# First layer of a two-layer decoder on one core: taps in one bank, skip row on TensorE, first pair first, diagonals on GpSimd

## The reference

```
scores = (x Wq)(ctx Wk)' / sqrt(32)          # 4 heads, 154 keys
top    = the 32 largest scores of each row; softmax over them, 0 elsewhere
c      = mean over heads (probs) @ (ctx Wv) * text_mask
u      = layernorm(x) * (1 + gate * scale_in(c)) + gate * shift_in(c)
K[d,l] = 2 Re sum_n dC[d,n] exp(dt[d] A[d,n] l),  l = 0..511      # the taps
y      = causal convolution of u with K (by FFT) + D_skip * u
out    = layernorm(x + film_out(y) + FFN(...))
```

## Time and profile before

| | us |
|---|---|
| median of 3 runs | 796.4 (796.21 to 798.48) |
| profiled execution, time | 798.87 |
| profiled execution, span on the core | 797.0 |
| TensorE matmuls busy in the span | 715.0 (90%) |
| VectorE busy | 456.8 (57%) |
| ScalarE busy | 279.4 (35%) |
| GpSimd busy | 225.4 (28%) |

### The profile page before, as it was taken

The page is one execution under the profiler, slowest core; times in us unless marked ns, Lnnn a source line. Parts: engine busy times, 40 slices in busy tenths (PEclk is TensorE's granted clock), DMA queues, the critical chain, the costliest instruction groups (busy, mean ns, idle before and its releaser), DMA issues.

```text
span 797.0 us, 8521 instructions
## 1 busy us (share of the span) xinstructions
PE 715.0 (90%) x3088; PEld 355.8 (45%) x3088; DVE 456.8 (57%) x1192; ACT 279.4 (35%) x527; POOL 225.4 (28%) x134
## 2 busy tenths in 40 slices
PE   8756869798989999999999999989968999999996
PEld 4223456774845443222222222228433354656555
DVE  7698973422635785576766767734664635333333
ACT  7799754003021003544444444430214103121220
POOL 4726910000200020445354545550725010000001
PEclk9757989999998999999999999999988969999999
DMA  8100050020000000000000000000500000000000
GB/s 313 32 0 0 1 211 2 1 81 27 1 0 1 0 1 0 0 1 1 0 1 1 1 0 1 0 1 1 225 0 1 1 0 0 2 1 1 0 1 27
DMA packets 3491, 18.64 MB, mean 23 GB/s; under 512 B 887, under 2 KB 2040, under 8 KB 2938
## 3 DMA queue, kind: packets, MB, share of 16 engines
q1 hardware_dynamic: 3450, 18.11, 5.9%
HBM read 17.58 MB, written 0.52 MB: 23 GB/s over the span
## 4 chain that ended last, share of the span: by engine, by line
PE 68%; DVE 14%; ACT 9%; issue 3%; POOL 3%; DMA 1%; POOLq 0%; DVEq 0%; SPq 0%; ACTq 0%
PE PS L1847 10%; PE PS L1330 7%; PE PS L1861 5%; DVE SB L1484 5%; PE PS L1314 4%; PE PS L1285 4%; PE PS L1298 3%; PE PS L217 3%; DVE SB L1233 2%; PE PS L1346 2%; PE PS L704 2%; PE PS L1368 2%; PE PS L1413 2%; PE PS L1645 2%; PE PS L1656 1%
## 5 line engine op out<-in xcount | busy, mean ns | idle before, releaser
L197 POOL TENSOR_TENSOR SB<-SB 128x4 f32<-128x4 f32 (+1 forms) x24 | 23.9, 996 | 374.4 <-DVE SB L181 374.3
L1467 POOL TENSOR_TENSOR SB<-SB 128x1024 f32<-128x1024 f32 x32 | 75.2, 2349 | 127.8 <-ACT SB L1437 127.7
L1484 DVE TENSOR_REDUCE SB<-PS 128x2 f32<-128x1024 f32 x64 | 78.5, 1226 | 52.7 <-PE PS L1298 52.7
L1437 ACT ACTIVATE SB<-PS 128x1024 f32<-128x1024 f32 x64 | 65.5, 1023 | 105.3 <-PE PS L1317 105.2
L217 PE MATMUL PS<-SB 128*128 128x512 f32 (+1 forms) x190 | 89.7, 618 | 8.3 <-ACT SB L536 6.7
L1847 PE MATMUL PS<-SB 128*128 128x512 f32 x176 | 83.9, 618 | 0.0
L1314 PE MATMUL PS<-SB 64*128 64x512 f32 x256 | 68.9, 616 | 0.0
L1330 PE MATMUL PS<-SB 128*64 128x512 f32 x256 | 67.8, 610 | 1.2 <-DVE SB L1521 1.2
L1927 DVE TENSOR_TENSOR SB<-SB,PS 128x512 f32<-128x512 f32 (+1 forms) x48 | 33.0, 688 | 53.9 <-PE PS L1847 50.0
L1517 DVE RECIPROCAL SB<-PS 128x512 f32<-128x512 f32 x16 | 53.7, 3358 | 17.6 <-PE PS L1346 17.6
L1885 ACT ACTIVATE SB<-PS 128x512 f32<-128x512 f32 (+1 forms) x48 | 28.6, 596 | 88.6 <-PE PS L1847 88.6
(11 more groups left out here) (355 smaller groups left out, 1145.7 us busy)
## 6 DMA issues: line engine op xcount, KB each, us to landing
SB<-exp SPq DMA_DIRECT2D x1, 4352.0 KB, 14.0
SB<-moe SPq DMA_DIRECT2D x1, 4096.0 KB, 12.1
SB<-dft SPq DMA_DIRECT2D x1, 2304.0 KB, 11.8
SB<-att SPq DMA_DIRECT2D x1, 2048.0 KB, 7.9
SB<-mix SPq DMA_DIRECT2D x1, 768.5 KB, 4.8
SB<-mix SPq DMA_DIRECT2D x1, 640.0 KB, 6.0
SB<-ssm SPq DMA_DIRECT2D x1, 602.0 KB, 7.0
SB<-lat SPq DMA_DIRECT2D x1, 585.0 KB
```

What stands on the lines that cost most here:

```text
L1437: act.activation(expd[i % 2][:, 1024 * u:1024 * u + 1024], bank(2 * (u % 2), 2), ACT.Exp).then_inc(sem("d_exp"), 1)
L1467: pool.tensor_tensor(half_sums[half], e[:, 0:1024], e[:, 1024:], ALU.add).then_inc(sem("d_half_sum"), 1)
L1484: dve.tensor_reduce(shift[i % 2][:, qt:qt + DK + 1:DK], two_heads(bank(4, 2)), AX_X, ALU.max, negate=True)\
```

## The change

- Taps: one matmul for each of the 128 channels, 32 stationary columns (low lags) by 16 moving ones (high lags), placed at column group 32 j of the array (j = d mod 4), all written to bank 3. Their waits for ScalarE's copies of gathers and films and the wait of `gather(5)` for the copies of the taps go. ScalarE's 16 copies read bank 3.
- Skip: GpSimd halves D early (`b_pool_pre`), and TensorE adds the row to tap 0 by one matmul of one partition in each of the 8 groups of the taps' spectrum, which moves from behind `gather(5)` to behind `gather(6)`.
- Selection: VectorE selects pair 0 before it finds the peaks of pair 2; ScalarE copies the second scores after the exponentials of pair 1. The last round writes to bank 2 only.
- Diagonals: GpSimd forms the four diagonals of a tile by one product, placed among its products of the taps. ScalarE's `b_act_spectrum` moves behind the loop.

```diff
@@ -352,7 +352,8 @@
     minus_max, total, share = Sel(NT * H_X), Sel(NT * H_X), Sel(NT * H_X)
     exp_ring, left_ring, prob_ring = Sel(8 * S2), Sel(4 * S2), Sel(8 * S2)
     all_exp, left, probs = ([a[:, S2 * i:S2 * i + S2] for i in range(n)] for a, n in ((exp_ring, 8), (left_ring, 4), (prob_ring, 8)))
-    diag = [Sel(128) for _ in range(4)]
+    diagonal = Sel(H_X * 128)
+    diag = [diagonal[:, 128 * h:128 * h + 128] for h in range(H_X)]
 
     scored = [d_tab[:, 0:H_X * S2], d_tab[:, H_X * S2:2 * H_X * S2]]
     attn0 = Sel(T)
@@ -466,13 +467,6 @@
         pool.wait_ge(sem("s_low_waves"), h + 1)
         pool.tensor_tensor(low_k[:, c], low_k[:, c], low_e[:, c], ALU.mult).then_inc(sem("s_low_products"), 1)
 
-    def b_dve_skip(dve, follow):
-
-        dve.wait_ge(sem("s_taps_copied"), 16)
-        dve.wait_ge(sem("small_in"), SMALL)
-        follow(dve.tensor_scalar(skip_line, skip_line, 0.5, None, ALU.mult))
-        dve.tensor_tensor(taps[0:1, 0:128], taps[0:1, 0:128], skip_line, ALU.add).then_inc(sem("s_taps_in"), 1)
-
     def b_act_spectrum(act):
 
         act.wait_ge(sem("s_taps_dft"), 1)
@@ -529,11 +523,11 @@
     def b_act_taps(act):
 
         act.wait_ge(sem("s_taps"), 1)
-        tp = PS[:, 2048:4096].rearrange("p (g j c q) -> p c g j q", j=4, c=4, q=4)
+        tp = bank(3).rearrange("p (g c q) -> p c g q", c=4, q=4)
         to = taps.rearrange("p (c g j) -> p c g j", c=4, j=4)
         for q in range(4):
             for j in range(4):
-                act.activation(to[32 * q:32 * q + 32, :, :, j], tp[32 * j:32 * j + 32, :, :, j, q], ACT.Copy)\
+                act.activation(to[32 * q:32 * q + 32, :, :, j], tp[32 * j:32 * j + 32, :, :, q], ACT.Copy)\
                    .then_inc(sem("s_taps_copied"), 1)
 
     def b_pe_values(pe):
@@ -620,6 +614,7 @@
         for h in range(2):
             pool.tensor_copy(m2[:, :, h, :], by_batch)
         follow(pool.tensor_copy(ones_low, ones[0:1, :]))
+        follow(pool.tensor_scalar(skip_line, skip_line, 0.5, None, ALU.mult))
         follow(pool.tensor_copy(text_mask, text_bytes))
         pool.tensor_scalar(text_mask, text_mask, 1.0 / H_X, None, ALU.mult).then_inc(sem("masks_in"), 1)
         pool.wait_ge(sem("masks_in"), 1)
@@ -668,24 +663,21 @@
 
         def taps_of_lags():
 
-            pe.wait_ge(sem("x_attn_in"), 2 * TAPS_AT)
-            pe.wait_ge(sem("x_film_in"), TAPS_AT - 1)
             pe.wait_ge(sem("s_low_products"), 5)
             pe.wait_ge(sem("s_factors"), 4)
-            for g in range(D // 4):
-                ins = pe.matmul(PS[:, 2048 + 4 * HIGH * g:2048 + 4 * HIGH * (g + 1)], low_k[:, 4 * LOW * g:4 * LOW * (g + 1)],
-                                high_r[:, 4 * HIGH * g:4 * HIGH * (g + 1)], start=True, stop=True)
+            for d in range(D):
+                j, g = d % 4, d // 4
+                ins = pe.matmul(bank(3)[32 * j:32 * j + 32, HIGH * g:HIGH * g + HIGH], low_k[:, LOW * d:LOW * d + LOW],
+                                high_r[:, HIGH * d:HIGH * d + HIGH], start=True, stop=True, tile_position=(0, 32 * j))
             ins.then_inc(sem("s_taps"), 1)
 
         def gather(t):
 
             if t >= 2:
                 pe.wait_ge(sem("x_attn_in"), 2 * (t - 1))
-            if t == TAPS_AT:
-                pe.wait_ge(sem("s_taps_copied"), 16)
             stay_warm(pe, 1, 4 + t % 2)
             pe.wait_ge(sem("x_probs"), 2 * t + 2)
-            pe.wait_ge(sem("x_diag"), H_X * t + H_X)
+            pe.wait_ge(sem("x_diag"), t + 1)
             o = bank(4 + t % 2)
             for h in range(H_X):
                 i = H_X * t + h
@@ -721,14 +713,15 @@
         def taps_spectrum():
 
             pe.wait_ge(sem("x_scores_in"), NT)
-            pe.wait_ge(sem("s_taps_in"), 1)
+            pe.wait_ge(sem("s_taps_copied"), 16)
             pe.wait_ge(sem("dft_in"), 16)
             for part, mat in ((0, dft["dft_cos"]), (1, dft["dft_sin"])):
                 for j in range(4):
+                    o = bank(part)[:, 128 * j:128 * j + 128]
                     for c in range(4):
-                        ins = pe.matmul(bank(part)[:, 128 * j:128 * j + 128],
-                                        mat[:, 512 * c + 128 * j:512 * c + 128 * j + 128],
-                                        taps[:, 128 * c:128 * c + 128], start=(c == 0), stop=(c == 3))
+                        ins = pe.matmul(o, mat[:, 512 * c + 128 * j:512 * c + 128 * j + 128],
+                                        taps[:, 128 * c:128 * c + 128], start=(c == 0), stop=False)
+                    ins = pe.matmul(o, mat[0:1, 128 * j:128 * j + 128], skip_line, start=False, stop=True)
             ins.then_inc(sem("s_taps_dft"), 1)
 
         score(0)
@@ -749,7 +742,7 @@
                     for j in range(4):
                         spectrum(0, j, 0)
                 film_tile(k)
-            if t == TAPS_AT:
+            if t == TAPS_AT + 1:
                 taps_spectrum()
         pe.wait_ge(sem("s_u_late"), 1)
         pe.wait_ge(sem("x_film_in"), NT)
@@ -776,7 +769,7 @@
             two = (2 * j, 2 * j + 1)
             m8 = [best[:, TOP * i:TOP * i + TOP] for i in two]
             base = 12 * j
-            rest = bank(2 + j % 2)[:, 0:2 * S2]
+            rest = bank(2)[:, 0:2 * S2]
             if j >= 2:
                 dve.wait_ge(sem("x_probs"), j - 1)
             for k, i in enumerate(two):
@@ -790,6 +783,8 @@
                     dve.wait_ge(sem("x_best"), base + 4 * r + k - 1)
                     if r == 3 and i == 0:
                         dve.wait_ge(sem("x_small_in"), 6)
+                    if r == 3 and j >= 1:
+                        dve.wait_ge(sem("x_probs"), j)
                     to = rest[:, S2 * k:S2 * k + S2] if r == 3 else left[i % 4]
                     ins = dve.match_replace(to, m8[k][:, 8 * r:8 * r + 8], left[i % 4], 0.0)
                     ins.then_inc(sem("x_selected" if r == 3 else "x_best"), 1)
@@ -801,7 +796,7 @@
             if i >= 8:
                 dve.wait_ge(sem("x_gathered"), i // 4 - 1)
             dve.tensor_tensor(prob_ring[:, S2 * (i % 8):S2 * (i % 8) + 2 * S2], exp_ring[:, S2 * (i % 8):S2 * (i % 8) + 2 * S2],
-                              bank(2 + j % 2)[:, 0:2 * S2], ALU.subtract).then_inc(sem("x_probs"), 1)
+                              bank(2)[:, 0:2 * S2], ALU.subtract).then_inc(sem("x_probs"), 1)
 
         def shares(t):
 
@@ -818,15 +813,15 @@
         peak(0)
         peak(1)
         for j in range(PAIRS_X):
-            if j + 2 < PAIRS_X:
+            if 0 < j < PAIRS_X - 2:
                 peak(j + 2)
             select(j)
+            if j == 0:
+                peak(2)
             if j % 2 == 0:
                 selected(j)
             else:
                 shares(j // 2)
-            if j == 14:
-                b_dve_skip(dve, follow)
 
     def b_act_attention(act):
         def scores_in(t):
@@ -847,17 +842,6 @@
                 act.activation(all_exp[i % 8], scores(i), ACT.Exp, bias=bias).then_inc(sem("x_exp"), 1)
                 act.activation(best[:, TOP * i:TOP * i + 8], peaks[:, 8 * i:8 * i + 8], ACT.Exp, bias=bias).then_inc(sem("x_exp"), 1)
 
-        def diagonals(t):
-            act.wait_ge(sem("x_sums"), 2 * t + 2)
-            act.activation(share[:, H_X * t:H_X * t + H_X], total[:, H_X * t:H_X * t + H_X], ACT.Copy, scale=text_mask[:, t:t + 1])\
-               .then_inc(sem("x_share"), 1)
-            act.wait_ge(sem("x_share"), t + 1)
-            if t >= 1:
-                act.wait_ge(sem("x_gathered"), t)
-            for h in range(H_X):
-                i = H_X * t + h
-                act.activation(diag[h], ident, ACT.Copy, scale=share[:, i:i + 1]).then_inc(sem("x_diag"), 1)
-
         def film_in(t):
             act.wait_ge(sem("x_film"), t + 1)
             if t == 0:
@@ -865,16 +849,12 @@
             act.activation(film[:, 512 * t:512 * t + 512], bank(6 + t % 2), ACT.Copy).then_inc(sem("x_film_in"), 1)
 
         scores_in(0)
-        scores_in(1)
         exponentials(0)
         b_act_film_inputs(act)
         exponentials(1)
+        scores_in(1)
         b_act_film_rows(act)
         for t in range(NT):
-            if t >= 1:
-                diagonals(t - 1)
-            if t == NT - 1:
-                b_act_spectrum(act)
             if t + 1 < NT:
                 exponentials(2 * t + 2)
             if t + 2 < NT:
@@ -896,7 +876,7 @@
                 b_act_low_rates(act, 16, LOW)
             if t == 3:
                 b_act_high_rates(act)
-        diagonals(NT - 1)
+        b_act_spectrum(act)
         film_in(NT - 2)
         attn_in(act, NT - 1)
         for k in FILMS[NT - 1]:
@@ -911,6 +891,18 @@
 
     def b_pool_attention(pool, follow):
         every_row = lambda a: a[:, None, :].to_broadcast([P, NT, 128])
+
+        def diagonals(t):
+            h = slice(H_X * t, H_X * t + H_X)
+            pool.wait_ge(sem("x_sums"), 2 * t + 2)
```

(27 more changed lines are left out.)

## The result

The changed kernel takes 805.3 us in the median, beside 800.1 us of the kernel before on the same chip: a ratio of 1.0061, with a 95% interval of 1.0040 to 1.0083, so 4.9 us slower (3.2 to 6.6). Six of its 20 executions (811.4 to 814.4 us) ran over 1.5% longer than its fastest and are left out of the ratio; without them the median is 804.8. The profiled execution took 805.25 us with a span of 803.5; the one of before 798.87 and 797.0.

What follows compares the result with a forecast made beforehand. VectorE's selection was taken to bound the stage's first half, TensorE's order its end from the taps on. +7.5 + 8.7 - 6.75 - 1.8 + 4.7 = +12.4 us gave 808.8 us, range 798 to 822.

Steps and rivals of the forecast that it cites:

- GpSimd's diagonals: First layer's cross-attention and filter: diagonals queue behind GpSimd's products, gathers wait, and the taps start 7.5 us later, at 108.3.
- Rival C: GpSimd is not in the way: gathers 1 to 3 not delayed, taps start at 100.8; 801.3 us, chance 0.10.
- The taps: TensorE: 256 loads and 256 small matmuls take 16.0 us (0.0625 each) against 7.33 now, +8.7, all on the path.
- Rival B: TensorE's column groups overlap: 7.2 us for the taps, +3.6 in all, 800.0 us; chance 0.13.
- Rival D: Small matmuls cost next to nothing (taps 3.5 us) and one-row matmuls hide (1.8): -3.0 us, 793.4 us; chance 0.10.
- The wait that goes: TensorE before the warming matmul at 114.68: ScalarE's copies no longer hold `gather(5)`, -6.75 us.
- The half clock behind the hole: Warming matmul and gather behind TensorE's removed wait no longer run at granted clock 0.50: -1.8 us.
- First pair first: VectorE's pair 0 starts 3.3 us earlier; some 2 us stay, eaten by the wait for `gather(1)`.
- Skip row: Taps' spectrum on TensorE: one-row matmuls add 0.59 us per group, 8 groups, +4.7 us on the path.
- The sum in the stage: First layer's cross-attention and filter: all terms together +12.4 us, L704's last piece starting at 159.3 against 146.9.
- The path from the stage to the end: What comes after L704's closing 96 instructions hangs on them and moves with them.
- rival A: Small matmuls go no faster than L1079's: 28.7 us for the taps, +25.1 in all, 821.5 us; chance 0.17.

Runs made afterwards that it cites:

- taps_twice: The changed kernel with the 128 matmuls of the taps done twice over, to the same places; 807.0 us in one execution.

## Why the prediction was right or wrong

The direction held, and the time (805.3) lies in the range. Two things make that look better than it is. I had forecast +12.4 us and it is +4.9; the 808.8 is near only because it starts from 796.4, while the kernel before took 800.1 beside the changed one. And 805.3 falls into the part of the range, 804 to 815, that I had tied to taps of 12 to 22 us. The taps took 4.7, under the 8 us below which I had called the prediction wrong. By its own test the mechanism of the largest term failed, and the nearness of the time is luck. By the steps:

- **GpSimd's diagonals: right.** Taps predicted from 108.3, measured 108.32; VectorE's two stalls predicted at 6.0 and 3.9, measured 6.13 and 4.14; diagonals out at 70.9 and 95.5, measured 69.5 and 94.3. Moving these calls in the order gave 16.4 us back. Rival C falls. The +7.5 is a net of a larger cost and of gains: against diagonals on ScalarE the late places cost 12.2 us, and early places on GpSimd would have gained 4.5. The 7.7 in the sum counts from the taps' starts; counted from the film tile ahead of them (107.27 against 98.74) the delay is 8.5, and the new taps start without the 0.73 us of issue ahead of the old ones.
- **The taps: wrong, the mis-sized term.** 16.0 us predicted, 4.7 measured; the term is not +8.7 but -2.6. I rated the instructions by the densest row I had, 0.07, in which each has 333 moving columns; that this number of columns bounds them is the prediction's reading, and no run tests it. Rival B's overlap is real: 0.009 each with four groups in turn, 0.031 with one. Its argument against, that there is little to overlap, was wrong: work of one group overlaps with that of the three others. At 4.7 us the case is between B (7.2) and D (3.5), and of all the sums B's, +3.6, is nearest to what the stage lost, +3.3; it had a chance of 0.13. The 62 ns for each matmul of the Trainium skill, "TensorE: Matmul & The Clock Gate", section "Wait — 56ns, not 53.3ns?", by which the taps would take an estimated 15.9 us, is not what this stretch shows; even the sustained 0.027 is under half of it. The page states them for decoding outside the hardware, and no trace here tells which decoding this is. The up to 4 times of "TensorEngine Tiling (Array Packing)", Theoretical Speedup, in the Trainium skill, fits the 3.4 seen here.
- **The wait that goes: right**, -6.75. No idle time of TensorE ends by the copies, and the old taps brought one of 6.72 back.
- **The half clock behind the hole: wrong.** The -1.8 were not earned: the clock fell behind the new taps as well, and the gather at 114.02 with its second half cost some 1.6 us more than at full clock. Warming matmul and gather together took 4.5 us, and 4.4 in the kernel before. Only with the taps in the order by group, without their pause, did the gather run at full clock.
- **First pair first: right as far as shown.** Some 2 us were predicted and to be eaten by the wait for `gather(1)`; the run without that wait shows 1.8.
- **Skip row: right.** +4.7 predicted, 12.0 us of spectrum predicted and measured, +4.9 when undone.
- **The sum in the stage** is then +7.7 - 2.6 - 6.75 + 0.3 + 4.7 = +3.3, where the 0.3 is what is left over, and the trace has 149.70 - 146.36 = +3.34. Rival D's condition (taps and skip rows together under 5.9 us) was not met: 4.7 + 4.7 = 9.4.
- **The path from the stage to the end: incomplete.** I let the rest move with the stage. In the profiled pair 3.1 us more arose behind it at a lower clock, and in the second profile of the changed kernel the span is 10.8 us over its counterpart, though its last spectra are only 1.6 us later. The mean granted clock of the 20 executions of the changed kernel lies between 0.929 and 0.953, with a median of 0.937; the kernel before had medians of 0.945 to 0.949 in its three later series. At like clocks the two are nearer than their medians, some 1 to 3 us apart: at 0.945 the changed one has a span of 800.1, the one before 798.9 to 799.1, and at 0.947 it is 799.9 against 796.8 to 797.2. So the changed kernel met the lower clock more often. Why isn't settled: the runs with early diagonals, which hold the same new taps, had medians of 0.950 to 0.957, and that the spectra ran at full or low clock in one and the same program (10.98 and 12.61) shows that it is not fixed by the instructions.

The 28.7 us of rival A for the taps were never near.

## What to carry to other kernels

Work moved to an idle engine inherits that engine's queue: look at what it will stand behind, and place each call before the long products whose results are needed later; here the order alone was worth 16 us, three times the whole effect of the change. Small matmuls in separate column groups were cheap here when neighbours alternated the groups: 4.7 us for 256 with their loads, and 7.9 with the groups one after the other. In a row twice as long the supply set the price, 0.027 us each. Two one-row instructions behind eight full ones cost 0.6 us, so a row sum of that kind belongs on an engine with time to spare. Judge such a change by the start of the next fixed piece as well as by the time, since the clock behind it can give or take as much as the change does.

## What the runs showed of the hardware

- A 32-column stationary with 16 moving columns: 0.009 us for load and matmul with four column groups in turn (the first 232), 0.031 in one group, 0.027 sustained over a longer run, with a pause of 1.6 to 2.3 us after the first 232 and after every 128 behind them (one profile, `taps_twice`).
- Two one-row fp32 instructions behind eight full ones add 0.6 us, where eight full ones take 0.9 (eight groups, 12.0 against 7.25 us).
- GpSimd multiplies 128x512 with two broadcast operands in 1.04 us, no more than the 1.10 of operands that aren't broadcast.
- A wait of TensorE of 2.1 us before 96 full matmuls left them at 10.98 in some executions and at 12.3 to 13.9 in others.
- The same work of one program, from the last spectra to L1078, took 65.9 us in one execution and 78.5 in another, and the stretch behind it 51.25 and 48.18, each time with the lower granted clock in the longer one (1.00 and 0.83, 0.87 and 0.93).
